# A gated cross-attention block with a routed FFN: a new hand-written order of the steps, with words that run early or late, and K of the first two batches moved inside SBUF

## What is computed

```python
x = x + tanh(g_xattn) * xattn(layernorm(x), ctx, ctx)      # 16 heads of depth 16
x = x + tanh(g_ffn) * ffn(layernorm(x))

def xattn(q, k, v):
    qh, kh, vh = split_heads(q @ wq + bq), split_heads(k @ wk + bk), split_heads(v @ wv + bv)
    attn = softmax(einsum('bhqd,bhkd->bhqk', qh, kh) / sqrt(16))
    return merge_heads(einsum('bhqk,bhkd->bhqd', attn, vh)) @ wo + bo

def ffn(x):                                                # F = 1024
    probs = softmax(x @ router_w)                          # 8 experts
    top, idx = top_k(probs, 2); top = top / top.sum(-1)
    combine = einsum('tk,tke->te', top, one_hot(idx))
    return (gelu(x @ w1 + b1) @ w2 + b2) * combine.sum(-1)
```

## Time and profile before

| | us |
|---|---|
| median of 3 runs | 801.17 |
| lowest, highest | 799.52, 803.07 |
| the profiled execution's own time | 803.36 |
| its span, first to last instruction | 801.6 |
| matmuls cover | 719.3 (90%) |
| DVE, ACT, POOL busy | 500.4, 393.2, 326.1 |
| mean granted TensorE clock | 0.976 |
| DMA: moved, mean rate | 104.73 MB, 131 GB/s |

### The profile page before, as it was taken

One profiled execution on the slowest core, in us unless ns is written; L12 is line 12 of the kernel. 1 busy time (PEld: TensorE's weight loads), 2 busy tenths in 40 slices (PEclk: granted clock), 3 DMA queues, 4 the chain that ended last, 5 costly groups with the idle time before them and its releaser, 6 DMA issues.

```text
span 801.6 us, 20546 instructions
## 1 busy us (share of the span) xinstructions
PE 719.3 (90%) x7648; PEld 663.4 (83%) x7648; DVE 500.4 (62%) x1297; ACT 393.2 (49%) x794; POOL 326.1 (41%) x478
## 2 busy tenths in 40 slices
...
GB/s 166 204 170 202 210 186 127 143 154 109 166 98 163 130 164 128 138 166 101 157 107 151 152 164 117 130 176 95 160 108 163 151 158 103 100 70 3 13 1 24
DMA packets 84820, 104.73 MB, mean 131 GB/s; under 512 B 9365, under 2 KB 80370, under 8 KB 84722
## 3 DMA queue, kind: packets, MB, share of 16 engines
...
...
HBM read 67.35 MB, written 35.59 MB: 128 GB/s over the span
## 4 chain that ended last, share of the span: by engine, by line
PE 58%; DVE 15%; POOL 10%; ACT 8%; issue 7%; DMA 1%; SPq 1%; POOLq 0%; DVEq 0%; ACTq 0%
PE P L848 27%; PE OT L900 9%; PE S L873 8%; PE T L885 8%; POOL HT_LO L529 5%; DVE NEGM L693 3%; PE P L926 3%; POOL HT_HI L527 3%; ACT KHI L589 2%; DVE KLO L701 2%; ACT L613 2%; DVE XT_LO L766 1%; ACT PROBS L613 1%; POOL RSTD L496 1%; DVE X L738 1%
## 5 line engine op out<-in xcount | busy, mean ns | idle before, releaser
L693 DVE TENSOR_REDUCE NEGM<-S 112x1 f32<-112x375 f32 x512 | 267.4, 537 | 54.1 <-PE S L873 50.6
L613 ACT ACTIVATE PROBS<-T 125x448 f32<-125x448 f32 x384 | 192.6, 543 | 140.1 <-PE T L885 136.8
L873 PE MATMUL S<-KS,QS 96*112 96x376 f32 x512 | 188.3, 371 | 11.8 <-DVE NEGM L693 9.9
L885 PE MATMUL T<-QS,KS 98*125 98x224 f32 x768 | 154.8, 284 | 7.4 <-ACT PROBS L613 6.0
L885 PEld LDWEIGHTS T<-QS,KS 98*125 98x125 f32 x768 | 128.3, 189 | 16.6 <-ACT PROBS L613 12.3
L873 PEld LDWEIGHTS S<-KS,QS 96*112 96x112 f32 x512 | 92.0, 180 | 25.3 <-DVE NEGM L693 22.9
L511 POOL CAST CT_HI<-CTRAW 128x750 fp32r<-128x750 f32 x32 | 27.3, 854 | 178.2 <-PE P L848 110.0
L542 POOL TENSOR_SCALAR XN<-B,WT 112x256 f32<-112x256 f32 x32 | 29.8, 931 | 159.8 <-DVE WT L817 156.4
L529 POOL TENSOR_TENSOR HT_LO<-HG,HT_HI 128x224 fp32r<-128x224 f32 x128 | 85.4, 667 | 10.3
L635 ACT ACTIVATE HG<-P,B 128x224 f32<-128x224 f32 x128 | 57.2, 448 | 46.2 <-PE P L848 31.7
L900 PE MATMUL OT<-PROBS,VA 125*17 125x112 f32 x3072 | 79.9, 259 | 0.0
...
## 6 DMA issues: line engine op xcount, KB each, us to landing
KS<-k_parts SPq DMA_DIRECT2D x96, 375.0 KB, 5.6
CTRAW<-in_ctxT SPq DMA_DIRECT2D x32, 375.0 KB, 6.7
k_parts<-KHI SPq DMA_DIRECT2D x32, 375.0 KB, 4.7
k_parts<-KLO SPq DMA_DIRECT2D x32, 375.0 KB, 5.2
QS<-q_parts SPq DMA_DIRECT2D x96, 112.0 KB, 4.0
...
q_parts<-QHI SPq DMA_DIRECT2D x32, 112.0 KB, 2.4
q_parts<-QLO SPq DMA_DIRECT2D x32, 112.0 KB, 2.3
```

Source lines behind the costliest of these rows:

```text
L613: act.activation(PT[0:KN, k, pp * 4 * SQ:(pp + 1) * 4 * SQ], T_BANK[i % 2][0:KN, 0:4 * SQ], ACT.Exp, scale=SCALE).then_inc(exp_done, 1)
L693: dve.tensor_reduce(NEGM[:, b.par, i:i + 1], S_BANK[i % 2][0:SQ, 0:SK], AX.X, ALU.max, negate=True).then_inc(max_done, 1)
L873: pe.matmul(S_BANK[i % 2][0:SQ, 0:SKP], QS[0:96, i, b.ring * SQ:(b.ring + 1) * SQ], KS[0:96, b.ring, i // 2, :], start=True, stop=True).th ...
L885: mm = pe.matmul(T_BANK[i % 2][0:KN, r * 2 * SQ:(r + 1) * 2 * SQ], KS[0:98, prv.ring, pair, k * KN:(k + 1) * KN], QS[0:98, 2 * pair:2 * pa ...
```

## The change

Three things change. First, a word may carry a suffix: `+n` runs it for the step's batch minus n (late), `-n` for the step's batch plus n (early), and the scores are numbered in the text. Second, all texts are new: the steady pair and the steps -2 to 5 and 32 to 35. In the steady pair both batches' K lie in the odd step, the P.V products of the even step's batch are moved to the front of the odd step, three S of the next batch are done before a step ends. P0 and P1 are dealt out by one plan over the whole run. Third, K of batches 0 and 1 (DIRECT = 2) goes from KHI and KLO straight into KS by DMA, four DMAs a strip, and the first context is split by ACT and DVE instead of POOL. The rest of the diff lets each engine use the batch of the word instead of that of the step.

```diff
 def stages(text):
-    out, head = [], 0
+    out = []
     for word in text.split():
+        word, _, late = word.replace("-", "+-").partition("+")
         name, _, i = word.partition(".")
-        if name == "s":
-            i, head = head, head + 1
-        out.append((name, int(i or 0)))
+        out.append((name, int(i or 0), int(late or 0)))
     return out
 ORDER = [stages(text) for text in (
-    """m ks kl cl qs xl ct mt s k.0 x2t s k.1 l1 s n1 up.0 s up.1 lo.0 n2 up.2 lo.1 s up.3 lo.2 up.4 lo.3 s
-       up.5 lo.4 up.6 lo.5 s up.7 lo.6 xn s rt lo.7 st.0 s rx xt st.1 v.0 st.2 s st.3 q.0 st.4 s q.1 st.5 s
-       st.6 wo st.7 s st.8 s v.1 st.9 s st.10 s st.11 v.2 pv.0 pv.1 pv.2 pv.3 au""",
-    """m ql ks kl cl ol ct mt s k.0 n1 s k.1 rw.0 s n2 rw.1 v.0 rw.2 s v.1 s rw.3 wo s st.0 rw.4 s st.1 rw.5
-       dh.0 rw.6 st.2 s rw.7 st.3 s dn.0 st.4 s st.5 s dh.1 st.6 s st.7 dn.1 st.8 s st.9 s s st.10 s st.11
-       v.2 pv.0 pv.1 pv.2 pv.3 au x2n xb""")]
+    """m s.1 s.2 xn ks au+1 up.1 mt s.3 up.2 s.4 up.3 cl s.5 n1 lo.0 up.4 s.6 lo.1 up.5 lo.2 s.7 up.6 n2 s.8
+       lo.3 up.7 lo.4 s.9 st.0 rt s.10 ct rx ct-1 v.0 st.1 s.11 kl xt st.2 lo.5 s.12 rw.0 cl-1 v.1 m-1 st.3
+       s.13 lo.6 st.4 v.2 st.5 lo.7 qs s.14 ks-1 ql-1 st.6 q.0 s.15 st.7 s.0-1 rw.1 st.8 rw.2 wo st.9 st.10
+       xb-1 s.1-1 q.1 rw.3 s.2-1 st.11 rw.4""",
+    """mt pv.0+1 pv.1+1 pv.2+1 au+1 rw.5+1 rw.6+1 pv.3+1 v.0 s.3 k.0 k.1 st.0 s.4 xl+1 st.1 s.5 dh.0+1
+       rw.7+1 st.2 st.3 n1 s.6 s.7 dn.0+1 n2 s.8 st.4 s.9 v.1 st.5 ol st.6 s.10 kl v.2 wo st.7 s.11 st.8
+       s.12 dh.1+1 st.9 s.13 x2n+1 st.10 dn.1+1 s.14 k.0-1 x2t-1 s.15 k.1-1 st.11 s.0-1 l1-1 pv.0 pv.1 pv.2
+       pv.3 up.0-1""")]
 
 
 SPECIAL = {k: stages(text) for k, text in (
...
     (-3, """"""),
+    (-2, """l1 xl-2 xn cl+1 qs cx wq xt wk q.0 kd.0 wv q.1 k.0 ct k.1 l1-2 xn-2 v.0 l1-4 ka.2 xt-2 kd.1 v.1 cl
+       ql-1 v.2 lw1 tg"""),
+    (-1, """k.0 k.1"""),
+    (0, """s.0 s.1 s.2 kd.0+1 v.0+1 s.3 s.4 v.1+1 q.0 s.5 ct+1 s.6 s.7 s.8 v.2+1 s.9 xn-2 q.1 s.10 s.11 s.12
+       s.13 s.14 s.15 w1 ka.2+1 wl"""),
+    (1, """mt cl+2 k.0+1 k.1+1 st.0 on+2 kd.1+2 s.0 s.1 st.1 qs+1 ct+1 s.2 v.0+1 on+1 xt-1 ct s.3 v.1+1 m on s.4
+       st.2 cl+1 st.3 k.0 s.5 ks+1 st.4 ql bo xb+2 s.6 st.5 pv.0 kl+1 ks s.7 lw2.0 m-1 v.2+1 st.6 s.8 v.0
+       s.9 st.7 s.10 ct-1 k.1 s.11 st.8 s.12 st.9 v.1 pv.1 s.13 s.14 pv.2 s.15 kl s.0-1"""),
+    (2, """mt ks s.1 s.2 s.3 s.4 st.10+1 s.5 s.6 st.11+1 k.0 cl+1 s.7 k.1 on kl s.8 st.0 pv.3+1 m-1 st.1 au+1
+       s.9 st.2 s.10 s.11 xb+1 st.3 n1 s.12 st.4 s.13 pv.0 qs st.5 s.14 v.2+1 st.6 lw2.1 s.15 s.0-1 v.0
+       s.1-1 pv.1 st.7 s.2-1 cl s.3-1"""),
+    (3, """mt w2.0 q.0+1 st.8+1 q.1+1 s.4 n2+1 pv.2+1 s.5 st.9+1 wo+1 ct s.6 st.10+1 v.1+1 st.11+1 s.7 xl+1
+       v.2+1 s.8 st.0 s.9 au+1 pv.3+1 s.10 s.11 st.1 st.2 k.0 n1 w2.1 ql k.1 st.3 lw2.2 s.12 xb st.4 ks v.0
+       n2 st.5 wr s.13 m-1 st.6 wo s.14 s.15 x2n+1 st.7 st.8 pv.0 st.9 v.1"""),
+    (4, """mt lw2.3 pv.1+1 st.10+1 s.0 st.11+1 l1 cl+1 w2.2 pv.2+1 s.1 s.2 x2t lo.0 k.0 s.3 k.1 s.4 pv.3+1 st.0
+       st.1 v.2+1 w2.3 st.2 st.3 s.5 ks s.6 rt up.0 s.7 xn up.1 s.8 up.2 au+1 s.9 up.3 lo.1 s.10 up.4 lo.2
+       s.11 up.5 s.12 st.4 s.13 v.0 n1 v.1 st.5 s.14 s.15 rx up.6 rw.0 up.7 rw.1 kl+1 st.6 ct rw.2 st.7 xl
+       s.0-1 rw.3 s.1-1"""),
+    (5, """mt pv.0+1 pv.1+1 s.2 k.0 st.8+1 rw.4+1 s.3 st.9+1 xt+1 k.1 st.10+1 s.4 lo.3+1 lo.4+1 lo.5+1 lo.6+1
+       s.5 kl+1 st.11+1 m lo.7+1 q.0+1 rw.5+1 pv.2+1 pv.3+1 au+1 ks rw.6+1 n2+1 q.1+1 st.0 s.6 n1 s.7 st.1
+       v.2+1 v.0 qs+1 st.2 s.8 st.3 cl+1 rw.7+1 s.9 wo+1 s.10 n2 v.1 st.4 wo s.11 st.5 s.12 ql kl dh.0+1
+       l1-1 st.6 s.13 cl st.7 pv.0 pv.1 s.14 x2n+1 dh.1+1 st.8 dn.0+1 st.9 dn.1+1 k.0-1 k.1-1 ct st.10 s.15
+       s.0-1 st.11 x2t-1 pv.2 pv.3 ol v.2 xb up.0-1"""),
+    (32, """up.1 lo.0 lo.1 lo.2 mt au+1 up.2 m up.3 up.4 up.5 rt st.0 st.1 rx rw.0 rw.1 rw.2 st.2 rw.3 st.3 n1
+       st.4 st.5 pv.0 rw.4 st.6 lo.3 ol-1 st.7 rw.5 pv.1 rw.6 st.8 st.9 n2 st.10 st.11 lo.4 rw.7 pv.2"""),
+    (33, """au+1 pv.3+1 ol-2 lo.5+1 up.6+1 lo.6+1 n1 wo+1 n2 lo.7+1 up.7+1 wo dh.0+1 x2n+1 dh.1+1 dn.0+1"""),
+    (34, """x2t dn.1+2 up.0 lo.0 up.1 up.2 lo.1 up.3 lo.2 up.4 lo.3 up.5 up.6 rt rx rw.0 lo.4 up.7 rw.1 rw.2 lo.5
+       rw.3 lo.6 lo.7 rw.4 dh.0 rw.5 rw.6 dh.1 rw.7 dn.0 dn.1"""),
+    (35, """"""),
 )}
 
 
-def banks(order):
+FIRST, LAST = -3, NB + LAG - 1
+
+
+BATCH = {"k": 2, "v": 2, "q": GB, "wo": -2, "up": -LAG, "dh": -LAG, "dn": -LAG}
+
+
+def order_of(k):
+    return SPECIAL.get(k, ORDER[k % GB])
+
+
+def bank_plan():
+
+    plan, last, kept = {}, 1, {}
+    for k in range(FIRST, LAST + 1):
+        for stage in order_of(k):
+            op, i, late = stage
+            if op not in BATCH or not 0 <= k - late + BATCH[op] < NB:
+                continue
+            if op == "dn":
+                plan[k, stage] = kept.pop(i)
+            else:
+                last = 1 - (next(iter(kept.values())) if len(kept) == 1 else last)
+                plan[k, stage] = last
+                if op == "dh":
+                    kept[i] = last
+    return plan
+
+
+BANKS = bank_plan()
...
+        def loads_of(b):
+            return 48 * ((b.k - DIRECT) // 2 + 1)
+
+        def move_k(engine, b, row):
+
+            part, moved = (KLO, klo_moved) if row == 1 else (KHI, khi_moved)
+            for p in range(4):
+                engine.dma_start(KS[32 * row:32 * row + 32, b.ring, p:NPAIR:4, 0:SK].bitcast(F32),
+                                 part[32 * p:32 * p + 32, :, :].bitcast(F32)).then_inc(moved[b.k], 16)
...
+                    if op == "kd":
+
+                        held(sp, sp_passed, (klo_done if i == 1 else khi_done, nn.count(2, 2)))
+                        move_k(sp, nn, i)
...
-                        held(sp, sp_passed, (ks_loaded, nn.count(48, -48)), (khi_done, nn.count(2, 2)))
+                        held(sp, sp_passed, (ks_loaded[nn.par], loads_of(nn) - 48), (khi_done, nn.count(2, 2)))
...
+                    if op == "ka":
+                        act.wait_ge(klo_done if i == 1 else khi_done, nn.count(2, 2))
+                        move_k(act, nn, i)
+                    if op == "cx":
+                        act.wait_ge(ct_loaded, 16)
+                        act.activation(CT[0][:, 0, :, 0:SK], CTRAW[:, :, :], ACT.Copy).then_inc(ct_hi_done, 1)
...
+                        if 0 < nn.k <= DIRECT:
+                            act.wait_ge(khi_moved[nn.k - 1], 2 * 4 * 16)
+                        elif nn.k > DIRECT:
+                            act.wait_ge(khi_stored, nn.count(16, -16 * DIRECT))
...
+                    if op == "cx":
+                        dve.wait_ge(ct_hi_done, 1)
+                        dve.tensor_tensor(CT[1][:, 0, :, 0:SK], CTRAW[:, :, :],
+                                          CT[0][:, 0, :, 0:SK].bitcast(F32), ALU.subtract).then_inc(ct_lo_done, 1)
...
-                            pe.wait_ge(ks_loaded, b.count(48, 48))
+                            if b.k < DIRECT:
+                                pe.wait_ge(khi_moved[b.k], 2 * 4 * 16)
+                                pe.wait_ge(klo_moved[b.k], 4 * 16)
+                            else:
+                                pe.wait_ge(ks_loaded[b.par], loads_of(b))
```

More of the change, by code:

```diff
@@ L362, in run @@
         def run(engine, step):
-            for k in range(-3, NB + LAG):
+            for k in range(FIRST, LAST + 1):
                 step(At(0, k))
@@ L496, in rstd, with step @@
                 pool.tensor_tensor(res[:, :], ve[:, :], MHALF[:, :], ALU.pow).then_inc(res_sem, 1)
-            def step(b):
-                ng, lg, pg = b.shift(GB), b.shift(-GB), b.shift(-LAG)
-                for op, i in b.order:
+                latest[0] = (res_sem, n)
+            def step(now):
+                for op, i, late in now.order:
+                    b = now.shift(-late)
+                    ng, lg, pg = b.shift(GB), b.shift(-GB), b.shift(-LAG)
                     if op == "bo":
@@ L556, in _, with step @@
         def _(act):
-            def step(b):
-                nn, prv, pp2 = b.shift(2), b.shift(-1), b.shift(-2)
-                ng, pg = b.shift(GB), b.shift(-LAG)
-                if b.k == 3:
-                    act.wait_ge(rest_loaded, 16 * N_REST)
-                for stage in b.order:
-                    op, i = stage
-                    bank = P_BANK[b.banks.get(stage, 0)]
+            def step(now):
+                for stage in now.order:
+                    op, i, late = stage
+                    b = now.shift(-late)
+                    nn, prv, pp2 = b.shift(2), b.shift(-1), b.shift(-2)
+                    ng, pg = b.shift(GB), b.shift(-LAG)
+                    bank = P_BANK[BANKS.get((now.k, stage), 0)]
                     if op in SPLIT:
```

99 lines of the change are left out of this document (44 added, 55 removed), and 3 rows, old and new, of the table SPECIAL.

## The result

The changed kernel takes 735.5 us (median of 4 executions, 735.24 to 740.0) against 802.12 us for the kernel before (median of 4, one execution more than in the table of before): a ratio of 0.9157, 95% interval 0.9086 to 0.9227. The forecast was 734 us, range 714 to 764. Its terms are another matter: two of the three are off, in opposite directions.

What follows compares the result with a forecast made beforehand. TensorE was taken to bound the steady pairs, 40.6 of 45.4 us being products and 4.8 waiting. Savings of 38 (steady), 19 (fill) and 10 (drain), 67 us from 803.36, gave 736.4, for the median 734 us; range 714 to 764.

Steps and rivals of the forecast that it cites:

- What bounds it: Twelve pairs of steps 6 to 29: TensorE's products sum to 40.6 us of 45.4 a pair, 4.8 us are waiting.
- The steady order: Steps 6 to 29: new word order cuts a pair to 42.2 us, saving 38 us over twelve pairs, from 16 to 48.
- 40.6 + 1.6: Steady pair: 40.6 us of products plus 0.7 for late maxima and 0.9 for short waits gives 42.2 us.
- The SP queue: Steady pair's in-order loads and stores: maxima's rows land about 1 us before st.0 of the odd step; no stall taken.
- Fill: Start up to step 6: 11.7 + 12 - 5 = 19 us saved, from 3 to 28.
- Hardly earlier now: Fill: six Q loads, issued at 22.62 to 25.69 before, land at 29.7; first S 11.7 us earlier.
- the loss falls from 30 to 18: First S to step 6: time lost to waits and clock falls by 12 us, with 5 given back.
- DMA: Before step 6: 115.5 us of busy DMA must fit in about 146, a share of 0.79, so data need not bind.
- The second rival: Fill bound by data: DMA share stays at 0.75, step 6 at 154 us, fill saves 5, total 748 us; chance 0.18.
- Drain: Steps 30 to the end: 10 us saved, from 4 to 15, of which 6 in steps 30 and 31.
- The sum: Whole kernel: 38 + 19 + 10 = 67 us saved from 803.36 gives 736.4, less 2.2 for the median: 734 us.
- The signs: Profile if right: about 42 us between like P.V bursts, first S near 30, step 6 near 146, DMA share near 0.8.

## Why the prediction was right, point by point

**What bounds it.** Right. 40.6 us of products by their spacing, in part an estimate; the changed kernel's full pair of 41.8 leaves 1.2.

**The steady order** (38 us): right in mechanism, off by 7 us, 2.1 of which are K of batch 8 on the other side of the mark. The term "40.6 + 1.6" put 0.7 us at s.5 and st.4 and 0.9 for short waits; together they are 1.2, of which 0.2 show as idle time. Why it works is less simple than "each wait is undone". Moving n2 alone gives nothing, mending three waits in the old order makes it slower by 2.0 us a pair (0.6 where the clock holds), and taking K's place back costs 1.0. Shown of the distribution over the two steps are K out of the step that holds the ups (12 us) and the ups one by one with an S between (3.7 us). The remaining 27 us or so, if these two add up, were not taken apart word by word; that they belong to the distribution too is argued, not shown.

**The SP queue.** Right that it must be counted and that it is the way to a slower kernel; the margin was too small in the forecast (1 us; some 3 measured), for it took the context's landing from an order in which K's loads went first. With the queue delayed a pair took 2.5 us more, 2.1 where the clock held.

**Fill** (19 us): wrong, 7.9 measured, inside its bounds of 3 to 28. Two steps failed. "Hardly earlier now" for the Q loads: the K moves ahead of them take SP 5.6 us to issue, 0.7 each where the forecast has 1.6 us for four, so they went out at 25.0 and not at 22.6, and the first S at 32.9 and not at 29.7; with the loads moved up it was 29.95. And "the loss falls from 30 to 18": from the first S on nothing was gained. Step 0 is a chain on DVE, shown by the eight maxima; its list was never added up in the forecast. Part of the rest is no loss: at the mark of step 6 the new order has already made K of batch 8 (2.1 us, missing again in the last steady pair) and two ups and three S (1.9 us, missing again in the drain), by the spacings of the forecast. The direct moves' share is 2 to 3 us of first S and nothing in the end.

**DMA.** The forecast had 115.5 us of DMA work before step 6 and a share of 0.79. Measured: 0.69 x 33.0 + 0.75 x 123.8 = 115.6 us, share 0.74. The second rival's numbers thus came true, a share near 0.75 and step 6 at 156.8 where it had 154, but its mechanism did not. With K through DRAM the stretch from the first S to step 6 carried a share of 0.82 instead of 0.75 and took no longer (121.1 us, 123.8), so data were not the bound there; and in step 0 eight more maxima moved step 1 by 5.8 us. The rule of the Trainium skill, "DMA: Bandwidth & Descriptors", section "Issuing engines are not separate DMA queues", says that moving issues to another engine saves only the issuing time, and that this is usually small beside the transfer. Here the issuing time counts: eight moves of 93.8 KB take SP 5.6 us to issue, more than the 4.9 us (median) in which one of K's high part lands. Taking four of them and a context load out of the way of the Q loads brought the first S 2 to 3 us forward.

**Drain** (10 us): 11.0 in the profiled execution, 14 at equal clock, some 2 of it the ups and S made ahead of the mark.

**The sum** came to 1.5 us of the median, and that close it is luck: the steady order gave 7 us more, the fill 11 less, and the clock in the drain decides over another 4.5.

**The signs.** Those for the steady order came (no idle time ahead of n2, the maxima's rows in time, DVE's maximum as releaser once a pair). Those for the fill did not: first S 32.9 and not near 30, step 6 at 156.8 and not near 146, DMA share 0.74 and not near 0.8.
